# One kernel for a four-layer attention and expert stack: a stage reordered, a query tile halved, result tiles signalled singly, the last sums moved into the tile block

## What is computed

```python
x = x + L0_ffn(L0_cond(x, ...))   # attention, then a ternary linear map
x = x + L1_ffn(L1_cond(x, ...))   # cosine attention; 8 experts, top 2, each takes at most 512 rows
x = x + L2_ffn(L2_cond(x, ...))   # 8 experts top 2 plus shared expert; then 8 experts, top 1, at most 256 rows
x = x + L3_ffn(L3_cond(x, ...))   # cosine attention; 8 experts, top 2, SwiGLU, no capacity
```

## Time and profile before

| | |
|---|---|
| median of the runs | 2162.24 us |
| the profiled execution | 2164.9 us, span 2163.1 us |
| PE busy | 1957.1 us, 90% |
| DVE busy | 1123.2 us, 52% |
| ACT busy | 963.6 us, 45% |
| POOL busy | 606.4 us, 28% |
| mean granted TensorE clock | 0.952 of full speed |

### The profile page before, as it was taken

One profiled execution on the slowest core, in us unless ns is written; L12 is line 12 of the kernel. 1 busy time (PEld: TensorE's weight loads), 2 busy tenths in 40 slices (PEclk: granted clock), 3 DMA queues, 4 the chain that ended last, 5 costly groups with the idle time before them and its releaser, 6 DMA issues. The chain is left out here.

```text
span 2163.1 us, 46615 instructions
## 1 busy us (share of the span) xinstructions
PE 1957.1 (90%) x16901; PEld 1493.1 (69%) x16901; DVE 1123.2 (52%) x3351; ACT 963.6 (45%) x2533; POOL 606.4 (28%) x917
## 2 busy tenths in 40 slices
PE   6999999988999999699989876998899999969995
PEld 3477777855677777466656655884567777859994
DVE  5388883275788834201026554117678884343333
ACT  2388882145888832111112331214678883211110
POOL 2022221067111114311116343116711111443332
PEclk9999999999999999799998986999989999979997
DMA  3095523000644221333322653631010004311114
GB/s 113 29 251 149 161 85 103 1 10 1 189 119 119 61 79 38 109 114 107 102 88 80 181 165 113 205 125 54 0 43 22 22 12 157 121 54 50 48 46 133
DMA packets 158675, 197.93 MB, mean 92 GB/s; under 512 B 15555, under 2 KB 132255, under 8 KB 158461
## 3 DMA queue, kind: packets, MB, share of 16 engines
q1 hardware_dynamic: 146024, 168.26, 25.6%
q0 software_dynamic: 11616, 26.26, 3.4%
q10 hardware_dynamic: 820, 0.57, 0.1%
HBM read 120.33 MB, written 88.64 MB: 97 GB/s over the span
## 5 line engine op out<-in xcount | busy, mean ns | idle before, releaser
L1052 ACT ACTIVATE att_pr<-all_h,att_nmax 128x512 f32<-128x512 f32 (+3 forms) x768 | 420.1, 550 | 14.6 <-DVE att_nmax L1004 14.6
L1118 PEld LDWEIGHTS att_t_ps<-all_ident,att_pr 64*128 64x128 f32 x3840 | 153.0, 139 | 60.7 <-DVE att_pt L1015 27.7
L2043 PE MATMUL exp_f_h_ps<-exp_f_xs_t,cw_f_w 128*128 128x512 f32 (+1 forms) x512 | 173.2, 498 | 1.5 <-DVE exp_f_xs_t L2081 1.5
L2055 PE MATMUL exp_f_y_ps<-cw_f_w,exp_f_hid 128*128 128x256 f32 x768 | 168.4, 380 | 0.0
L1118 PE MATMUL att_t_ps<-all_ident,att_pr 64*128 64x64 f32 x3840 | 163.6, 224 | 1.2 <-DVE att_pt L1015 0.5
L2111 ACT ACTIVATE exp_f_hid<-exp_f_h_ps 128x512 f32<-128x512 f32 (+1 forms) x128 | 62.4, 490 | 216.5 <-PE exp_f_h_ps L2043 216.5
L2055 PEld LDWEIGHTS exp_f_y_ps<-cw_f_w,exp_f_hid 128*128 128x128 f32 x768 | 145.2, 191 | 19.2 <-issue 0.5
L967 POOL COPY att_rexp<-att_rinv 128x512 f32<-128x512 f32 x96 | 58.6, 610 | 354.7 <-DVE att_rinv L1019 280.8
L2271 PEld LDWEIGHTS til_f_ab_ps<-til_f_xs_t,til_f_now 128*128 128x128 f32 x1248 | 146.8, 194 | 5.3 <-DVE til_f_xs_t L2338 3.5
L2271 PE MATMUL til_f_ab_ps<-til_f_xs_t,til_f_now 128*128 128x128 f32 x1248 | 147.3, 277 | 2.9 <-POOL til_f_now L2226 2.3
L1066 ACT ACTIVATE att_pt<-att_t_ps 128x1024 f32<-128x1024 f32 x120 | 122.9, 1024 | 58.1 <-PE att_t_ps L1118 58.1
(11 more groups left out here) (412 smaller groups left out, 4064.1 us busy)
## 6 DMA issues: line engine op xcount, KB each, us to landing
sorted_c<-all_zero SPq DMA_DIRECT2D x8, 2056.0 KB, 13.1
sorted_f<-all_zero SPq DMA_DIRECT2D x8, 2056.0 KB, 11.7
cw_f_w<-in_L_ffn_w_dram SPq DMA_DIRECT2D x16, 1024.0 KB, 8.7
cw_f_w<-in_L_ffn_W_dram SPq DMA_DIRECT2D x12, 1024.0 KB, 7.2
band<-rev SPq DMA_DIRECT2D x2, 4096.0 KB, 18.4
tw_f_wab<-in_L_ffn_w_dram SPq DMA_DIRECT2D x2, 4096.0 KB, 20.3
tw_c_xs<-sorted_c SPq DMA_DIRECT2D x39, 128.5 KB, 2.8
sorted_f<-all_zero SPq DMA_DIRECT2D x8, 514.0 KB, 4.9
```

The lines of the kernel that those rows point to most:

```text
L1052: nc.scalar.activation(pr[u % 4][:, hh, at], sc[u % 4][:, hh, at], ACT.Exp, scale=-1.0, bias=nmax[:, b, q, h:h + 1], accum_out=rsum[:, b, ...
L1118: last = nc.tensor.transpose(t_ps[e % 2][:, half, WIDE * hh + kb, :], pr[u % 4][d, hh, P * kb:P * (kb + 1)], c.ident[d, d])
L2043: last = nc.tensor.matmul(h_ps[f % 4][:, 0:cap], w1_sb[n][:, k, P * f:P * (f + 1)], xs_t[n][:, k, :], start=(k == 0), stop=(k == KD - 1))
L2055: last = nc.tensor.matmul(y_ps[(YT * n + t // 2) % 2][:, t % 2, :], hid[n][:, f, P * t:P * (t + 1)], w2_sb[n][:, f, :], start=(f == 0), st ...
```

## The change

Five edits:

1. In `combine_and_relate`, DVE and PE take their pieces in another order.
2. In `attention_inputs` with cosine scores, query tile 15 is projected, copied, squared, summed, raised, multiplied, transposed and copied out as two halves of 8 heads.
3. In `experts_by_capacity`, each result tile has a bank, a copy and a signal of its own, and POOL scatters it alone; POOL's last round is written out with constants.
4. `Combine` loads batch 0 as two halves of two tiles, and sums it in these halves, in every stage that uses it.
5. The final block is gone: all loads of the last sum are issued at the end of the tiles' block, which also sums and stores; the last batch is stored in two halves.

```diff
 # attention_inputs: DVE, for t == LAST (15); ACT, POOL and PE are split in the same way
+        def sum_last(n):
+            dve.wait_ge(last_squared, n + 1)
+            nc.vector.tensor_reduce(qn[:, LAST, heads(n)], sq[LAST % 2][:, heads(n), :], AX.X, ALU.add).then_inc(last_summed, 1)
+            dve.wait_ge(last_summed, n + 1)
+            nc.vector.tensor_scalar(qn[:, LAST, heads(n)], qn[:, LAST, heads(n)], 1e-24, None, ALU.max).then_inc(last_floored, 1)
+        def keep_last(n):
+            dve.wait_ge(last_copied, n + 1)
+            dve.wait_ge(last_root, n + 1)
+            q = q_sb[LAST % 4][:, heads(n), :]
+            nc.vector.tensor_tensor(q, q, qn[:, LAST, heads(n)].unsqueeze(2).to_broadcast([P, H // 2, DH]), ALU.mult).then_inc(last_kept, 1)
...
-                    sum_q(t)
+                    if t == LAST:
+                        sum_last(0)
+                        sum_last(1)
+                    else:
+                        sum_q(t)
...
-            keep_q(NT - 1)
+            keep_last(0)
+            keep_last(1)
 # PE
+                if t == LAST:
+                    last.then_inc(last_ready, 1)
...
-            for t in (NT - 2, NT - 1):
-                turn_q(t)
+            turn_q(NT - 2)
+            turn_last(0)
+            turn_last(1)
 # experts_by_capacity, PE
                 for t in range(CT):
-                    if t % 2 == 0:
-                        pe.wait_ge(y_copied, i * (2 * YT) + max(YT * n + t // 2 - 1, 0) + 1)
+                    pe.wait_ge(y_copied, i * (2 * CT) + max(CT * n + t - 1, 0) + 1)
...
-                    if t % 2:
-                        last.then_inc(y_ready, 1)
+                    last.then_inc(y_ready, 1)
 # DVE
-                for y in range(YT):
+                for t in range(CT):
...
-                    nc.vector.tensor_copy(ys[n][:, 2 * y:2 * y + 2, :], y_ps[(YT * n + y) % 2][:]).then_inc(y_copied, 1)
+                    nc.vector.tensor_copy(ys[n][:, t, :], y_ps[(CT * n + t) % 2][:, 0, :]).then_inc(y_copied, 1)
 # POOL, after a loop of R - 1 rounds
+            for n in range(2):
+                pool.wait_ge(idx_copied, 2 * (R - 1) + n + 1)
+                for t in range(CT):
+                    pool.wait_ge(y_copied, (R - 1) * (2 * CT) + CT * n + t + 1 + 1)
+                    scatter(n, t)
 # Combine
+            if b == 0:
+                for half, loaded in zip(self.halves, self.half_loaded):
+                    for k, t, rows in half:
+                        sp.dma_start(rows, self.by_batch[b][:, k, t:t + 2, :]).then_inc(loaded, 16)
...
+        if b == 0:
+            for n, (half, loaded) in enumerate(zip(self.halves, self.half_loaded)):
+                dve.wait_ge(loaded, 16 * len(half))
+                for k, first, rows in half:
+                    if k:
+                        dve.wait_ge(self.half_added, 2 * (n + 1))
+                    self.add(k, first, rows)
 # experts_by_tile, SP and DVE, where out is given (layer 3)
+                for b in range(B):
+                    step = QT if b + 1 < B else 2
+                    for at in range(0, QT, step):
+                        sp.wait_ge(com.added, QT * b + at + step)
+                        sp.dma_start(out[b, P * at:P * (at + step), :].rearrange("(t p) d -> p t d", p=P),
+                                     c.x[:, QT * b + at:QT * b + at + step, :]).then_inc(out_stored, 16)
+                sp.wait_ge(out_stored, 16 * (B + 1))
...
+                for b in range(B):
+                    com.vector(dve, b)
 # combine_and_relate, DVE
         part.vector_ahead(dve, 2)
+        part.vector(dve, 2)
+        part.vector_ahead(dve, 3)
         rel.second_hidden(dve)
         rel.statistics(dve, 1)
-        part.vector(dve, 2)
-        part.vector_ahead(dve, 3)
+        part.vector(dve, 3)
         rel.normalise(dve, 1)
-        part.vector(dve, 3)
         rel.scale(dve, 1)
 # combine_and_relate, PE
         part.tensor(pe, 2)
-        rel.product(pe, (0, 1))
-        rel.product(pe, (2, 3))
         part.tensor_turn(pe, 3)
         part.tensor_after(pe, 2)
+        rel.product(pe, (0, 1))
         part.tensor(pe, 3)
+        rel.product(pe, (2, 3))
         part.tensor_after(pe, 3)
 # build
-            com = Combine(nc, c, f3, done["f3"], r_f3, c.x, c.x, inner, soon=2, pairs=result_rows)
-            experts_by_tile(nc, c, f3, kept3[0], done["f3"], r_f3, com)
-            with stage(nc) as (stack, block):
...
+            com = Combine(nc, c, f3, done["f3"], r_f3, c.x, c.x, inner, soon=B, pairs=result_rows)
+            experts_by_tile(nc, c, f3, kept3[0], done["f3"], r_f3, com, out=out)
```

More of the change, by code:

```diff
@@ L766, in project_q, with turn_last @@
                     last = nc.tensor.matmul(q_ps[t % 2][:, n, :], c.xt[:, k, P * t:P * (t + 1)], wq[:, k, S * n:S * (n + 1)], start=(k == 0), stop=(k == KD - 1))
-            last.then_inc(q_ready, 1)
+                if t == LAST:
+                    last.then_inc(last_ready, 1)
+            if t != LAST:
+                last.then_inc(q_ready, 1)
+        def turn_last(n):
+            pe.wait_ge(last_kept, n + 1)
+            if n == 0:
+                pe.wait_ge(qt_copied_a, LAST)
+            for i in range(HP // 2 * n, HP // 2 * (n + 1)):
+                last = nc.tensor.transpose(qt_ps[:, i, :], q_sb[LAST % 4][:, 2 * i:2 * i + 2, :].rearrange("p h d -> p (h d)"), c.ident[:])
+            last.then_inc(last_turned, 1)
         def turn_q(t):
@@ L2149, in place_down, with experts_by_tile @@
         self.loads_d = [(self.wd[:, e, :, :], self.weight_d[e].rearrange("(k p) f -> p k f", p=P), self.wd_loaded) for e in range(E)]
[L2152 removed]
+def experts_by_tile(nc, c, mx, tw, expert_rows, r, com, ahead=(), soon=(), rel=None, out=None):
     F = mx.hidden
@@ L2212, in _ @@
             com.sync(sp)
+            if out is not None:
+                for b in range(B):
[5 more added lines that the diff above has]
+                sp.wait_ge(out_stored, 16 * (B + 1))
         def kept_weights(expert, k):
@@ L2406, in __init__ @@
         self.pieces = [[(k, 0, rows[b][:, k, :, :]) for k in range(max(own, 1))] + ([] if spare is None else [(1, t, ap) for t, ap in spare(b)]) for b in range(B)]
+        self.halves = [[(k, at, ap[:, at - t:at - t + 2, :]) for k, t, ap in self.pieces[0] if t <= at < t + ap.shape[1]] for at in range(0, QT, 2)]
+        self.half_loaded = [m.sem(f"half_loaded{n}") for n in range(2)]
         self.loaded = [m.sem(f"loaded{b}") for b in range(B)]
@@ L2417, in load @@
         for b in batches:
-            for k, t, rows in self.pieces[b]:
-                sp.dma_start(rows, self.by_batch[b][:, k, t:t + rows.shape[1], :]).then_inc(self.loaded[b], 16)
-    def vector(self, dve, b):
-        top = self.mx.top
-        dve.wait_ge(self.loaded[b], 16 * len(self.pieces[b]))
-        for k, first, rows in self.pieces[b]:
-            if k:
-                dve.wait_ge(self.half_added, QT * (b + 1))
-            for t in range(rows.shape[1]):
-                at = QT * b + first + t
-                self.nc.vector.scalar_tensor_tensor(out=self.dst[:, at, :], in0=rows[:, t, :], scalar=self.r.weight[:, k, at:at + 1],
-                                                    in1=(self.dst if k else self.start)[:, at, :], op0=ALU.mult,
-                                                    op1=ALU.add).then_inc(self.added if k == top - 1 else self.half_added, 1)
+            if b == 0:
+                for half, loaded in zip(self.halves, self.half_loaded):
+                    for k, t, rows in half:
+                        sp.dma_start(rows, self.by_batch[b][:, k, t:t + 2, :]).then_inc(loaded, 16)
+            else:
+                for k, t, rows in self.pieces[b]:
+                    sp.dma_start(rows, self.by_batch[b][:, k, t:t + rows.shape[1], :]).then_inc(self.loaded[b], 16)
@@ new lines, in vector @@
+    def vector(self, dve, b):
+        if b == 0:
[5 more added lines that the diff above has]
+                    self.add(k, first, rows)
+        else:
+            dve.wait_ge(self.loaded[b], 16 * len(self.pieces[b]))
+            for k, first, rows in self.pieces[b]:
+                if k:
+                    dve.wait_ge(self.half_added, QT * (b + 1))
+                self.add(k, QT * b + first, rows)
@@ L2434, with add @@
+    def add(self, k, first, rows):
+        for t in range(rows.shape[1]):
+            at = first + t
+            self.nc.vector.scalar_tensor_tensor(out=self.dst[:, at, :], in0=rows[:, t, :], scalar=self.r.weight[:, k, at:at + 1],
+                                                in1=(self.dst if k else self.start)[:, at, :], op0=ALU.mult,
+                                                op1=ALU.add).then_inc(self.added if k == self.mx.top - 1 else self.half_added, 1)
 class SharedWeights:
```

78 lines of the change are left out of this document (48 added, 30 removed).

## The result

The changed kernel takes **2148.86 us** (median of 5 runs, 2141.09 to 2149.32), the kernel before 2162.32 in runs beside it (2161.78 to 2164.81): ratio 0.9926, 95% interval 0.9911 to 0.9942. It is 13.5 us faster; forecast were 16.8.

A forecast was written before the change was run, and what follows sets the result against it. The prediction took chains at stage handovers, run while PE is idle, as the bound. Gains 3.1 + 1.0 + 1.7 + 4.2 + 6.0 + 0.8 = 16.8 us against the 2162.24 median gave 2145.4 us, range 2140 to 2152.5.

The forecast's parts named there:

- The 1.0 in the stage behind layer 1's experts: Edit 4's forecast gain there from loading and summing batch 0 in halves: 1.0 us, bounds 0 and 1.6.
- Rival E: Batch 0's halves land together, since they share one queue: 1.7 + 1.0 less 0.5, total 2147.6 us; chance 0.11.
- the signs: Listed observations that would show the forecast, among them normalising about 6.5 us sooner after the third sum stage's start.
- Rival A: Third sum stage: the clock rises as late or later in the new order; 3 us less, 2148.4 us; chance 0.13.
- Rival C: Third sum stage: the new order helps nothing, only the start gain stays; 2149.6 us; chance 0.09.
- B: Last query tile of attention inputs: pow of a half costs nearly a whole; 2151 us; chance 0.06.
- The 5.5 and 8.4 among the signs: Attention inputs were to end 5.5 us and not 8.4 after tile 14's pow.
- The lag of 0.3: Final sums: DVE finishes batch 0 early but waits for batch 1, so only its lag of 0.3 us goes.
- Rival D: Capacity experts: wait before each result tile no longer covered, PE takes turns with DVE's copy; slower, 2168 us; chance 0.03.

The follow-up runs named there:

- the other sets: The unaltered changed kernel measured again in two further sets of runs against the kernel before: 2146.23 us (ratio 0.9918) and 2147.69 us (0.9934).
- paired tiles: Changed kernel with edit 3 undone (two result tiles share a bank, a copy and a signal): 2149.60 us, ratio 0.9946.
- last tile whole: Changed kernel with edit 2 undone in all four engines: 2154.01 us, ratio 0.9959.

## Why the prediction was right, and where it was not

The sum was 16.8, the medians give 13.5 (15.0 and 16.1 in the other sets), and the forecast's direction and range held. Term by term:

| edit | forecast | shown | by |
|---|---|---|---|
| 3, single tiles | 3.1 | 3.2 at the scatters, 2.5 in the stages | before and after; paired tiles |
| 1, order | 4.2 | 4.9 | 55.57 to 50.71 with whole batches |
| 2, last query tile | 6.0 | 6.2 (5.3 to 6.1 undone), and perhaps 1.9 in layer 3's attention | 3.18 + 2.98; last tile whole |
| 5, end | 0.8 | 0.45 | 22.36 to 21.91 |
| 4, halves | 2.7 | about -1 | below |

With 3.2 this sums to 13.7, and to 15.6 with the attention; the profiled pair differs by 16.0. That 16.0 comes so near 16.8 is in part luck: edit 4 was taken 3.7 too high, and layer 3's attention gave 1.9 that was not forecast.

**Edit 4 is the step that failed.** The prediction said that the second half lands "at +5.3 as now" and that batch 1 "lands when it did". In six profiles with batch 1 queued behind, the second half landed at 5.8 to 7.0 in the third sum stage, and in the end, over seven, batch 1's first sum started at 9.0 to 10.4 in place of 8.6. The first half did come early (2.75 and 3.46 us after the first issue, where 3.8 was forecast); that only moved the pause behind it. To that come the issues that the prediction called covered by the wait for data: the barriers are later by 0.23, 0.4 and 0.46 us after the first issue, and since in the third sum stage the first half is there by then (the bracket of the sum at 1277.42 names PE's sequencer at the barrier, not a DMA), they now count. Taken together: -0.2, -0.35 and -0.5 at three barriers, 0 to +0.9 in the third stage (49.85 to 50.56 in five profiles with halves, 50.59 and 50.71 with whole batches), -0.4 to -1.9 in the end. The -1 of the table is an estimate from these; no median shows it. The 1.0 in the stage behind layer 1's experts fell for another reason, PE's twelve warming matmuls; the prediction counted on such matmuls before layer 3's inputs and left them out here. Rival E came nearest, but left the halves 0.5 of gain. The rule to coalesce (the Trainium skill, page DMA: Bandwidth & Descriptors, section Rules for kernel authors) was weighed only against the last store, where it did not bite: that store of 256 KB landed 2.14 us after its issue (forecast 2.2), against 2.92 for 512 KB. The estimate of 2.75, by the 2.0 us of that page's section Anatomy of one DMA in the Trainium skill, was too high; the section is on DMAs issued from GpSimd, and this store is issued from SP. A price of smaller transfers showed on the loads.

**Edit 1** came out as reasoned, a little more: wait for the root 0.32, scaling at once, last row 4.87 sooner. Normalising started 4.18 sooner after the stage's start, where the signs say 6.5; the working itself gives 5.2 (1324.91 less 1319.7), of which 1.7 were to come from the halves and did not. With whole batches it is 3.8 (42.20 to 38.41), and batch 3's positions, now in the root's wait, give the other 1.1. Rival A's condition was nearly met, its price was not: the clock rose 29.0 us after the stage's start, 29.5 before, but batch 3's logits began just behind that and took 1.85 and the product's second half 1.97, both at the full level; the first half took 2.73, and the network's last product 3.60 for 3.22, all in the price of 4.9. Rival C is out.

**Edit 2** came out as summed, by other pieces. The last pow ends 3.2 us behind tile 14's, where 3.9 were forecast (4.84 before): 8 columns take 1.63, not 1.94, so B is out by far. But the last tile's transposes wait until ACT has copied tile 14 (534.47 to 535.50), so 3.1 us pass behind the last pow, where 2.5 were forecast (4.56 before). Together 6.3 for 9.4; the sum forecast 6.4. The 5.5 and 8.4 among the signs leave out the 1.04 that POOL idled behind tile 14's pow (539.37 less 531.00 is 8.4) and can't be held against this. The 1.9 in the attention was not foreseen.

**Edit 3** and **edit 5** were right at the place named; in edit 5 the forecast let the halves help, which they did not, and the clears at the very end take 0.82 us (0.59 with whole batches), 0.41 before. The lag of 0.3 was not won: with whole batches DVE's last sum ended 18.71 us after the first issue, 18.59 before; the 0.45 is the shorter last store less the clears and this. **Rival D** is out: PE 220 of 220 us.

**The two heaps.** The stage behind layer 1's experts lasted 76 us in both profiles of the changed kernel and 69.9 to 78.5 over all; in the three profiles read for it the clock goes with it. Its stretch from 10 to 45 us after the start, in the changed kernel and in the one with paired tiles (69.86 us):

```profile
1130.54:1165.54 35.00, 33.02 (x143) 22.01 (x142) 23.82 (x90) 9.86 (x18) 22.57 (x22) 0.85 0.24 85
```

```profile
1131.11:1166.11 35.00, 33.44 (x160) 21.85 (x159) 26.88 (x106) 12.13 (x23) 22.95 (x23) 0.95 0.26 90
```

0.80 in the kernel before (77.01), 0.85 (75.94), 0.95 (69.86). The first attention stage does the same in one and the same kernel: 239.67 and 237.33 us, with 0.66 and 1.00 of the clock in its first 10 us:

```profile
102.70:112.70 10.00, 8.38 (x41) 3.80 (x40) 4.70 (x13) 5.73 (x13) 2.01 (x8) 0.66 1.00 285
```

```profile
102.70:112.70 10.00, 7.71 (x69) 4.52 (x69) 6.17 (x17) 7.86 (x17) 2.22 (x9) 1.00 0.98 291
```

The Trainium skill, page TensorE: Matmul & The Clock Gate, section Part 1: The HAM clock gate (the "warmup" mystery), says that the matmuls at the low clock differ in number between runs of one kernel; the traces agree, with 0.66 and 1.00 in the same stretch of the same kernel. No run of the changed kernel near 2141 was profiled. Of the variants, the three whose profiled execution took 2141.1 to 2142.3 had this stage at 69.9, 71.8 and 72.9; all others, from 2145.2 up, had it at 74.7 or more. That the heap near 2141 is the fast stage fits this and is not shown.

## What to carry to other kernels

To start on part of the data sooner, first give each transfer that is already there its own semaphore; cutting transfers smaller costs issues ahead of a barrier and delays everything queued behind. Price a split by what the later pieces and the next batch do, not by the first landing, and look on every engine for what already covers the wait, filler matmuls too. Where the clock's level moves whole runs by more than the edit, compare stage lengths and rows, and undo edits in pairs.

## What had not been expected of the hardware

- Pow on POOL took 1.63 us for 128x8, 2.9 to 3.9 for 128x16 (median 3.8 of 30) and 1.00 for 128x4: at this place two halves, 3.26, were cheaper than the whole's 3.81.
- Loads of 256 KB: the first landed 2.6 to 2.9 us after its issue, 512 KB after 3.8 to 4.0; but the third and fourth of a row came late, 4.5 to 5.0 and 5.3 to 7.1, and the rate was 223 to 270 GB/s between 3.5 and 5 us after the first issue, 360 to 363 with 512 KB.
- The granted clock in the first 25 us of layer 3's attention was 0.74, 0.86 or 1.00, and 239.66, 237.75 and 235.28 us went with it. The 0.86 and the 1.00 stood in kernels with the same stage ahead.
